# Where four conversions of the value cache, half a batch's key pages and the output weights' late conversions stand in an attention kernel

## The reference, cut to what matters

```python
x = x + einsum('bct,bcd->bdt', x, weights[subjects])          # 32 samples, 32 x 512 each
q, k, v = x @ Wq.T, x @ Wk.T, x @ Wv.T                        # 32, 8 and 8 heads of 128
q, k = rope(rmsnorm(q, q_norm_w), pos), rope(rmsnorm(k, k_norm_w), pos)
kc, vc = k_cache[block_table], v_cache[block_table]           # 16 pages of 32 keys a sample, from 64 pages
k_all, v_all = concat([kc, k]), concat([vc, v])               # 512 + 32 keys
probs = softmax(where(valid, q @ k_all.T * SCALE, -1e30))     # 4 query heads share a key head
x = x + (probs @ v_all).reshape(...) @ Wo.T
```

## Time and profile before

| what | value |
|---|---|
| runs before | 1003.75, 1003.89 and 1002.6 us, median 1003.75 |
| the profiled execution | 1004.66 us, its span 1002.9 us |
| PE busy | 960.4 us (96%) |
| DVE busy | 830.8 us (83%) |
| ACT busy | 754.3 us (75%) |
| POOL busy | 581.8 us (58%) |
| mean granted TensorE clock | 0.997 |

### The profile page before, as it was taken

One profiled execution on the slowest core, in us unless ns is written; L12 is line 12 of the kernel. 1 busy time (PEld: TensorE's weight loads), 2 busy tenths in 40 slices (PEclk: granted clock), 3 DMA queues, 4 the chain that ended last, 5 costly groups with the idle time before them and its releaser, 6 DMA issues.

```text
span 1002.9 us, 25118 instructions
## 1 busy us (share of the span) xinstructions
PE 960.4 (96%) x8075; PEld 797.4 (80%) x8075; DVE 830.8 (83%) x1845; ACT 754.3 (75%) x2104; POOL 581.8 (58%) x859
## 2 busy tenths in 40 slices
PE   6899999999899999899999999999999999989998
PEld 4678888888677778688888888888888888878885
DVE  7789999999998688888878878888887787877880
ACT  5798999988784688877767777777777777777760
POOL 5555665655893068756655665565556655655550
PEclk9899999999999999999999999999999999999999
DMA  5799999989998979999999999999999999999950
GB/s 197 274 305 340 320 385 370 385 280 386 394 348 256 383 272 361 332 290 253 303 305 268 292 290 293 302 285 284 320 261 274 330 284 262 318 285 269 270 127 11
DMA packets 249907, 294.92 MB, mean 294 GB/s; under 512 B 79024, under 2 KB 206512, under 8 KB 247216
## 3 DMA queue, kind: packets, MB, share of 16 engines
q1 hardware_dynamic: 231088, 226.07, 76.0%
q0 software_dynamic: 18688, 67.25, 18.2%
HBM read 231.77 MB, written 46.27 MB: 277 GB/s over the span
## 4 chain that ended last, share of the span: by engine, by line
PE 71%; DVE 16%; issue 4%; ACT 3%; POOL 3%; DMA 2%; DVEq 0%; SPq 0%; ACTq 0%; POOLq 0%
PE ps_y L1530 16%; PE ps_proj L1530 15%; PE ps_o L1611 14%; PE ps_s L1568 8%; PE ps_t L1582 7%; PE ps_s L1572 7%; DVE probs L1264 2%; PE ps_rt L1706 2%; DVE c_stage L1426 2%; DVE rot L1402 2%; DMA vs<-v_pages,v_row 2%; DVE stage L1412 2%; DVE rot L1394 2%; PE ps_o L1623 1%; DVE pt L1284 1%
## 5 line engine op out<-in xcount | busy, mean ns | idle before, releaser
L1036 ACT ACTIVATE probs<-probs,neg_max 128x544 f32<-128x544 f32 x256 | 191.5, 748 | 139.6 <-DVE neg_max L1264 123.7
L1264 DVE CUSTOM_DVE_ANT_0 probs<-ps_s,mask,row_scale 128x544 f32<-128x544 f32 x256 | 200.3, 782 | 48.9 <-PE ps_s L1572 34.2
L1611 PE MATMUL ps_o<-pt,vs 128*128 128x128 f16 x3072 | 213.3, 219 | 1.1 <-DMA vs<-v_pages,v_row 1.1
L1611 PEld LDWEIGHTS ps_o<-pt,vs 128*128 128x128 f16 x3072 | 192.7, 98 | 15.7 <-DMA vs<-v_pages,v_row 1.6
L960 POOL TENSOR_SCALAR probs<-probs,recip 128x512 f32<-128x512 f32 x144 | 100.1, 695 | 169.6 <-DVE recip L1272 166.7
L906 POOL TENSOR_TENSOR roped<-rot 128x256 f32<-128x256 f32 x160 | 145.2, 929 | 81.5 <-DVE rot L1394 76.2
L1530 PE MATMUL ps_proj<-wt_hi,x0t_hi 128*128 128x512 f32 x384 | 159.6, 417 | 6.2 <-DVE x0t_lo L1220 5.7
L1284 DVE SCALAR_TENSOR_TENSOR pt<-ps_t,pt 128x512 f16<-128x512 f32 x190 | 130.2, 685 | 41.3 <-ACT pt L1042 33.0
L1530 PE MATMUL ps_y<-wo,ot_hi 128*128 128x512 f16 x512 | 153.5, 381 | 2.7 <-DVE ot_lo L1301 2.7
L1530 PE MATMUL ps_proj<-wt_hi,x0t_lo 128*128 128x512 f32 x384 | 151.1, 395 | 0.0
L1530 PE MATMUL ps_proj<-wt_lo,x0t_hi 128*128 128x512 f32 x384 | 150.3, 393 | 0.0
(11 more groups left out here) (162 smaller groups left out, 1807.7 us busy)
## 6 DMA issues: line engine op xcount, KB each, us to landing
kt<-k_pages_t SPq DMA_DIRECT2D x512, 128.0 KB
c_nat<-in_L_cond_k_cache SPq DMA_DIRECT2D x32, 512.0 KB, 6.0
q_t<-stage SPq DMA_DIRECT2D x64, 256.0 KB, 6.4
c_nat<-in_L_cond_v_cache SPq DMA_DIRECT2D x32, 512.0 KB, 7.1
qt<-q_t SPq DMA_DIRECT2D x32, 512.0 KB
w_nat<-in_L_cond_Wq SPq DMA_DIRECT2D x8, 1024.0 KB, 7.7
k_pages_t<-c_stage SPq DMA_DIRECT2D x16, 512.0 KB, 5.3
c_nat<-in_L_cond_Wo SPq DMA_DIRECT2D x16, 512.0 KB, 6.7
```

The costliest lines, as they stand in the source:

```text
L1036: act.activation(pr, pr, ACT.Exp, bias=col(neg_max, i), scale=-1.0, accum_out=col(row_sum, i)).then_inc(a_exp, 1)
L1264: dve.tensor_tensor_reduce(out=probs_of(i), in0=ps_s[:, score_cols(i):score_cols(i) + KEYS], in1=mask[(i // HK) % 2][:, mask_at(i):mask_at ...
L1611: ins = pe.matmul(ps_o[n % 2][:, jl * P:(jl + 1) * P], v[:, part, :], pt[pt_slot(i)][:, NCH * half + c, :], start=jl == 1 and c == 0 and k ...
```

## The change

Three edits of tables and one of `load_pages`' places.

1. The last four value conversions (28 to 31) come behind all scans in `TASKS`, and units 66, 69, 72 and 75 get no task. The list now ends in unit 82: conversions 28 to 31 stand in units 79, 80, 81 and 82.
2. `NEXT_KEYS_AT` is 85. Eight pages of batch 1 are issued in units 85 to 92, and the other eight right behind the last store of a value unit, after the loop.
3. The fourth chunk of the output weights is no longer loaded in unit 91; the fourth and fifth are issued together behind those eight pages, and the wait for all stores comes after them.
4. `WO_LATE` starts at step 16 instead of step 4, and `on_pool` picks remainders 1 and 6 instead of 0 and 6.

```diff
-    KEYS_AT, NEXT_KEYS_AT, PREFETCH, NEW_V_AT = 54, 80, 87, 93
-    WO_LOADS = {84: 0, 86: 1, 88: 2, 91: 3}
+    KEYS_AT, NEXT_KEYS_AT, PREFETCH, NEW_V_AT = 54, 85, 87, 93
+    WO_LOADS = {84: 0, 86: 1, 88: 2}
...
-    WO_LATE = (4, 8, 12, 16, *(20 + 12 * k // 5 for k in range(HQ - WO_EARLY - 4)))
+    WO_LATE = (16, 17, 20, 24, 25, 28, *(HK * k + r for k in (4, 5, 6) for r in (0, 1, 4, 6)), 56, 57)
...
-             + [("scan", n) for n in WO_SCANS[:7]] + mixed(V_CONVS, WO_SCANS[7:]))
+             + [("scan", n) for n in WO_SCANS[:7]] + mixed(V_CONVS[:-4], WO_SCANS[7:])
+             + [("conv", n) for n in V_CONVS[-4:]])
...
+    TASK_FREE = (66, 69, 72, 75)
+    TASK_UNITS = [TASK_AT + t // 2 for t in range(2 * PAIRS)] + [
+        u for u in range(TASK_AT + PAIRS, NU) if u not in TASK_FREE]
     for t in range(len(TASKS)):
-        TASK_IN[TASK_AT + t // 2 if t < 2 * PAIRS else TASK_AT + t - PAIRS].append(t)
+        TASK_IN[TASK_UNITS[t]].append(t)
...
-        return n >= WO_EARLY and (WO_LATE[n - WO_EARLY] + 1) % HK in (1, HK - 1)
+        return n >= WO_EARLY and WO_LATE[n - WO_EARLY] % HK in (1, HK - 2)
...
-                if NEXT_KEYS_AT <= u < NEXT_KEYS_AT + NPP:
+                if NEXT_KEYS_AT <= u < NEXT_KEYS_AT + NPP // 2:
                     load_pages(1, u - NEXT_KEYS_AT, 1)
...
+            load_pages(1, NPP // 2, NPP // 2)
+            load_wo(3)
+            load_wo(4)
             all_stored(sp)
             sp.wait_ge(d_x0, 16)
-            load_wo(len(WO_LOADS))
             load_new_v(1)
```

## The result

| what | before | after |
|---|---|---|
| median of the runs | 1002.98 us (1001.16 to 1003.89, 6 runs) | 1010.41 us (1008.79 to 1012.28, 6 runs) |
| ratio | 1 | 1.0073, 95% interval 1.0061 to 1.0086 |
| the profiled execution, its span | 1004.66, 1002.9 us | 1011.81, 1010.0 us |

The account below looks back on a forecast made before the run. Key units were taken as bound by VectorE, value units by PE. 4.2 - 0.4 + 0.5 = 4.3 us gain gave 1000.4 us profiled, 999.5 against the median; range 996.8 to 1003.0.

Parts of the forecast that it names:

- Part 1: Key and value units: moving four conversions later shifts VectorE work to PE-bound units; worth 4.2 us.
- The gate: Product 85 must wait for VectorE's low part of unit 82; forecast to start at 313.2 instead of 317.85, 4.6 us earlier.
- VectorE's 3.0 us: Sum of VectorE's savings before product 85: 1.54 + 0.5 + 1.3 - 0.3 us.
- The idle 1.3 us: VectorE's idle 0.45 us before unit 81 and 0.87 before the reciprocal, expected to vanish.
- rival A: Key units hurry but VectorE's backlog before product 85 stays as large; gain 1.6 us or less, 1002; chance 0.17.
- the slack of unit 85's wait: SP waits for all conversions in unit 85 instead of 80; about 3 us slack, costed at nothing, called not safe.
- Rival D: SP's stall at unit 85 delays queries or row scales beyond the first scores; no change; chance 0.05.
- Part 2: Eight key pages behind the last value store: a wait of 0.4 us at step 8's scores.
- The landing of 3.2 us: Time for a key page behind the last store to land, taken from value stores in the quiet window 350 to 358 us.
- The upper bound: Longest page wait at step 8's scores, with a loaded-window landing of 7.7 us: 4.9 us.
- Part 3: Attention steps: later output-weight conversions spare up to 1.4 us early, cost up to 1.5 late; gain taken as 0.5.
- B: Page wait at step 8's scores, in step 5, takes the gain's place, up to 4.9 us; slower or even; chance 0.08.

Follow-up runs that it names:

- p1_only: Kernel before with only the value conversions moved as in the change, all sixteen batch 1 pages still ahead of attention, two a unit from unit 85; ratio 1.0053.
- heads_late: Changed kernel with output-weight heads 8 to 11 converted at steps 2, 4, 8 and 12 instead of units 93 and 94; ratio 1.0025.
- p23_only: Changed kernel with the value conversions back where they were before; 1007.3 us, ratio 1.0029.
- best_c: all_ahead with output-weight chunk 0 in unit 81, chunks 3 to 7 later, and heads 8 to 11 at steps 2, 4, 8 and 12; 999.13 us, ratio 0.9953.
- best_d: p3_only with output-weight chunks 3 to 7 loaded later and heads 8 to 11 converted at steps 2, 4, 8 and 12; ratio 0.9981.
- pages_only: p3_only with eight of batch 1's pages behind the last value store, output-weight chunks as before; 1006.3 us, ratio 1.0025.
- p3_only: Kernel before with only the late output-weight conversions shifted (WO_LATE and on_pool as changed); ratio 0.9973.
- all_ahead: p1_only with the late output-weight conversions shifted and VectorE's row-scale chain in unit 82; 1001.8 us, ratio 0.9984.
- wo0_early: Changed kernel with output-weight chunk 0 (1 MB) issued in unit 81 instead of unit 84; ratio 1.0025.
- chain_later: Changed kernel with VectorE's row-scale chain one unit later, in unit 82 behind conversion 31; ratio 1.0009.
- p1_heads: p1_only with the late output-weight conversions shifted as changed and heads 8 to 11 converted late; 1007.3 us, ratio 1.0031.

## Why the prediction was wrong

**Part 1, VectorE and PE: right in kind, too big.** The gate stands where I put it. Product 85 waits 0.86 us for `stage`, not 2 to 5, and PE's waits for the turned heads fall to 3.8 us, not to 2. Conversions 29 to 31 take 1.27 to 1.28 us, as I had taken. From the fixed point product 85 starts at 102.8 us in place of 105.8, 3.0 us earlier, not 4.6; at product 93 it is 2.5 in the profiled execution and 3.4 in nearly all other runs with the conversions moved. I had 4.2. Compared from the start of the span it looks like 317.85 - 313.24 = 4.6 us, just what I had forecast, but by luck: 1.7 of that is a faster start-up and no gain. The term that was too big is VectorE's 3.0 us. It is through the gate 1.5 us earlier in this trace (104.1 and 102.7 us from the fixed point) and 2.4 in p1_only's. The idle 1.3 us that I struck out came back in part, as rival A said: the changed kernel has 0.27 us of idle time ahead of conversion 30 and a wait for GpSimd's scale that was not there before,

```profile
280.68 1.66 DVE L1408 SCALAR_TENSOR_TENSOR rot<-ps_proj,rstd,rope_k 128x256 f32<-128x256 f32 x4 [0.88 <-POOL rstd L936]
```

so that VectorE's idle time up to the gate is 4.2 us in place of 4.1, where my sum had 1.0 less.

**Part 1, SP: the step that failed.** "SP now waits for all conversions ... I see about 3 us of slack and cost it at nothing; DMA engines are full ..., so this is not safe." I looked at the slack of unit 85's wait. The wait that counts is the store of conversion 31 itself, in unit 82, behind the row scales on VectorE, 5.2 us on an in-order queue, with GpSimd's 2 MB of gathers tied to the same store. With engines that are full before and behind it, a hole of 4 us is traffic that lands later. The order of VectorE's work, which stood ahead of the prediction, showed conversion 31 behind the row scales. I used that to count what lies before the gate, not what waits for it. Measured, the conversions' part costs 5.3 us. PE had won 3.4 at product 93, so 8.7 were lost behind it; p1_only's trace shows 6.9 of them, ahead of the first maximum. Rival D had the mechanism, but ended it at "no change": it may cost more than PE had gained, because the same transfers hold ScalarE and VectorE as well, and because of the clock.

**Part 2: the landing.** The issue came out as worked out: pages from 1.26 us after the last store on, 0.5 us each. The landing of 3.2 us was taken from a quiet stretch; with the gathers beside it it is 6.1. Those gathers are in the trace of before, at the same steps, the first of them

```profile
355.75 1.02 POOL L941 DMA_INDIRECT vs<-v_pages,v_row  x1 [0.15 <-issue]
```

and I did not look whose transfers fill the window that I called quiet. The upper bound, a wait of 4.9 us, was the right end (3.0 in the changed kernel, 4.75 in heads_late). The estimate from the Trainium skill, DMA: Bandwidth & Descriptors, Anatomy of one DMA, was 2.3 us for a page; that section gives its fit for transfers issued through GpSimd, these pages are issued by SyncE, and the shortest landing of one that I could read in a trace here is 3.2 us. "... eight pages and one chunk of weights, some 2 MB, makes room ...; I cost that at nothing": behind the loop the two chunks hold up the pages of batches 2 and 3 by 1.9 and 1.5 us in p23_only's trace, but the timed runs show no cost of it. Part 2 costs 5.6 us by the runs, where I had 0.4, and nearly all of it is there with the late pages alone.

**Part 3: right in sign, too small.** 2.7 us in place of 0.5. I had priced GpSimd's waits, and left out that VectorE's masked maximum is late for the same early conversions (2.0 to 0.4 us).

**The rivals.** B and D both happened, and had 0.13 together. The rows for D stood in the prediction: an in-order queue that waits longer, and engines that are full. The sign that I gave for D, over 2 us at step 0's scores ended by a DMA, didn't show: that wait was 1.34 us, and the long one, 4.16, ended with VectorE's maximum. B's price for step 8's wait, up to 4.9 us, covers the 2.7 to 4.75 measured.

**What stays open.** best_c and best_d, like pages_only and p3_only, differ less in their single traces than in the timed runs; a trace shows one execution, and for p23_only and p3_only it was the slowest of the runs. No run moves GpSimd's gathers of batch 0 without SP's stall. The stretch behind the first output product ends within 578.4 to 580.7 us in all runs; I ascribe nothing to that.

## What to carry to other kernels

When a step moves later on one engine, follow its result to the queue that issues from it: an in-order queue passes the delay to everything behind. Look, too, what other transfers start on the same signal. Where the DMA engines were already full, the idle gap came back as a wait until 1 MB was moved into it or the stall was taken out. Price a transfer's landing with the traffic that will run beside it, another engine's gathers included, and not with the nearest quiet row. Compare two traces from a fixed instruction ahead of the change, since the start-up alone moved by 3 us here.

## What the runs showed of the hardware

The clock makes a wait dearer than its length. Behind PE's idle 4.16 us the granted clock of 343 to 353 us was 0.69, between its two levels of 1.2 and 2.4 GHz, and product 95 took 4.92 us in place of 2.7 to 2.8; with a wait of 5.68 us (p1_only) it was 0.67, with 3.14 us (all_ahead) and 2.30 us (wo0_early) 0.83, with 1.70 us (chain_later) and with none (heads_late) 1.00. The window doesn't lie alike behind each wait, so these are no curve. Where it does lie right behind one, the clock is at its lower level: p1_heads, whose PE had been idle for 4.85 us up to 357.78 and was busy from there on:

```profile
358.00:363.00 5.00, 5.00 (x30) 4.24 (x30) 2.22 (x5) 2.06 (x5) 3.79 (x5) 0.50 0.88 288
```

And best_c, where PE's wait of 2.11 us ended at 352.59 and the clock stayed at 1.00:

```profile
343.00:353.00 10.00, 7.34 (x50) 5.34 (x49) 6.99 (x20) 6.95 (x15) 4.25 (x6) 1.00 0.91 310
```

An issue can take long by itself: SP's issue of the queries took 3.47 us in the changed kernel, the next one 0.67; before it took 0.33. The DMA engines were full in both (shares of 1.01 and 1.03 from 326 to 330 us), so their share alone doesn't explain it; what does is not shown.

A conversion on VectorE, whose inputs both lie in SBUF, took 1.27 to 1.28 us in units 80 to 82 of the changed kernel, where GpSimd is nearly idle, and 1.54 on average from 246 to 309 us of the kernel before, where GpSimd is busy 55.31 of 63 us.
